# POOL issues eight scatters and then eight gathers, in place of four and four

## What is computed

```python
row, col = src, dst
edge_input = concatenate([x[row], x[col], edge_attr], axis=-1)
h = silu(edge_input @ eW1 + eb1)
m_ij = silu(h @ eW2 + eb2)
agg = segment_sum(m_ij, row, num_segments=50000)
update = silu(concatenate([x, agg]) @ nW1 + nb1) @ nW2 + nb2
out = layernorm(x + (x + update))
```

## Time and profile before

| | |
|---|---|
| median of 3 runs | 1614.44 us (1608.35 to 1617.39) |
| the profiled execution: time, span | 1598.11 us, 1596.6 us |
| mean granted TensorE clock | 0.923 of full speed |
| busy share of the span | PE 82%, DVE 59%, ACT 28%, POOL 65% |
| gathers L340, scatters L381 | 392 and 392 indirect DMAs on POOL, 999 and 1010 ns each |
| edge stage, as the copies of q (L776) stand in the trace | 132.7 to 1254.3 us |

### The profile page before, as it was taken

One profiled execution on the slowest core, in us unless ns is written; L12 is line 12 of the kernel. 1 busy time (PEld: TensorE's weight loads), 2 busy tenths in 40 slices (PEclk: granted clock), 3 DMA queues, 4 the chain that ended last, 5 costly groups with the idle time before them and its releaser, 6 DMA issues.

```text
span 1596.6 us, 24603 instructions
## 1 busy us (share of the span) xinstructions
PE 1304.5 (82%) x7491; PEld 886.1 (56%) x7491; DVE 937.9 (59%) x2976; ACT 443.4 (28%) x766; POOL 1043.0 (65%) x956
## 2 busy tenths in 40 slices
PE   1109888888888888888888888878999699999996
PEld 1005554454454454545455455545666499998995
DVE  9104554554554554554554555546677388888886
ACT  0001111111111111111111111111222177777776
POOL 8763666666666666666666666663443488887885
PEclk9558999999999999999999999998999899999998
DMA  9995333333333333333333333332333499999995
GB/s 379 410 413 172 99 100 106 102 99 101 107 98 102 109 98 106 101 101 105 99 105 101 102 103 102 101 107 81 106 111 94 156 358 383 383 381 365 382 384 227
DMA packets 156842, 284.94 MB, mean 178 GB/s; under 512 B 28046, under 2 KB 92322, under 8 KB 156708
## 3 DMA queue, kind: packets, MB, share of 16 engines
q1 hardware_dynamic: 110020, 162.78, 31.3%
q10 hardware_dynamic: 21600, 68.32, 10.6%
q0 software_dynamic: 25088, 52.23, 10.2%
HBM read 188.31 MB, written 94.91 MB: 177 GB/s over the span
## 4 chain that ended last, share of the span: by engine, by line
PE 31%; DVE 28%; another core or an unknown queue 28%; issue 8%; SPq 4%; DMA 1%; POOL 0%; ACT 0%; ACTq 0%; POOLq 0%
DVE junk L761 14%; PE psum L549 9%; PE psum L559 6%; DVE onehot L753 6%; PE psum L546 5%; DVE pick L743 4%; DVE xsT L734 2%; PE psum L488 2%; PE psum L502 1%; PE psum L505 1%; PE psum L525 1%; SPq L275 1%; PE psum L514 1%; PE psum L530 1%
## 5 line engine op out<-in xcount | busy, mean ns | idle before, releaser
L340 POOL DMA_INDIRECT x_src<-x_d,idx_src x392 | 391.5, 999 | 269.3 <-PE psum L476 149.2
L381 POOL DMA_INDIRECT table<-q,pos x392 | 395.9, 1010 | 199.7 <-issue 113.7
L761 DVE CUSTOM_DVE_ANT_0 junk<-onehot,psum 128x625 f16<-128x625 f16 x392 | 299.1, 800 | 74.2 <-PE psum L505 62.2
L776 DVE COPY q<-psum 128x512 f32<-128x512 f32 x98 | 67.8, 692 | 459.8 <-remote 425.7
L502 PE MATMUL psum<-onehot,after 128*128 128x512 f16 (+1 forms) x780 | 183.9, 320 | 155.1 <-DVE rank L761 153.6
L488 PEld LDWEIGHTS psum<-pick,window 128*128 128x128 f32 x1568 | 201.4, 200 | 95.3 <-issue 95.3
L488 PE MATMUL psum<-pick,window 128*128 128x128 f32 x1568 | 198.7, 282 | 33.7 <-issue 33.7
L502 PEld LDWEIGHTS psum<-onehot,after 128*128 128x128 f16 x780 | 55.2, 100 | 283.0 <-issue 268.8
L505 PE MATMUL psum<-onehot,before 128*128 128x512 f16 (+1 forms) x784 | 187.1, 324 | 0.0
L441 POOL TENSOR_TENSOR rstd<-var_eps,minus_half 128x5 f32<-128x5 f32 (+1 forms) x79 | 134.5, 1703 | 74.0 <-DVE var_eps L821 74.0
L590 ACT ACTIVATE hT<-psum,b_e 128x512 f32<-128x512 f32 x98 | 67.3, 687 | 401.5 <-remote 184.1
(11 more groups left out here) (92 smaller groups left out, 1520.9 us busy)
## 6 DMA issues: line engine op xcount, KB each, us to landing
window<-x_d SPq DMA_DIRECT2D x392, 128.0 KB
slots_in<-table SPq DMA_DIRECT2D x79, 528.0 KB, 6.2
table<-empty ACTq DMA_DIRECT2D x9, 4224.0 KB
x_in<-x_d SPq DMA_DIRECT2D x78, 320.0 KB, 5.1
xT_in<-xT_d SPq DMA_DIRECT2D x78, 320.0 KB, 5.2
out<-y_out ACTq DMA_DIRECT2D x78, 320.0 KB, 5.4
place<-place_dram SPq DMA_DIRECT2D x98, 128.0 KB
x_src<-x_d,idx_src POOLq DMA_INDIRECT x392
```

What stands on the lines that cost most here:

```text
L340: pool.indirect_dma_start(rows, None, x[:, :], bass.IndirectOffsetOnAxis(ap=idx[:, g * TILES + t:g * TILES + t + 1], axis=0)).then_inc(don ...
L381: pool.indirect_dma_start(table[:, :], bass.IndirectOffsetOnAxis(ap=pos[:, g * TILES + t:g * TILES + t + 1], axis=0), q[g % Q][:, t, :], None,
L761: V.tensor_tensor_reduce(out=junk[t % 2][:], in0=onehot[g % 2][:, t, :], in1=p_rank[t % 2], scale=-step if t % 2 else step, scalar=0.0, op ...
```

## The change

In the taken branch POOL goes through the groups in pairs: the scatters of groups g and g + 1, then the gathers of groups g + 22 and g + 23.

```diff
-                for g in range(GROUPS):
-                    scatter(g)
-                    gather_src(g + LEAD)
+                for g in range(0, GROUPS, 2):
+                    for h in range(g, min(g + 2, GROUPS)):
+                        scatter(h)
+                    for h in range(g, min(g + 2, GROUPS)):
+                        gather_src(h + LEAD)
```

## The result

The changed kernel takes 1770.34 us (median of 4 runs, 1767.29 to 1779.0) where the kernel before takes 1612.58 (4 runs): the ratio is 1.0986, with a 95% interval of 1.0935 to 1.1037. It is slower by 158 us; the prediction said 1750, slower by 144.

What follows compares the result with a forecast made beforehand. The prediction took POOL's unbroken runs of indirect DMAs, delaying PE's signals, as the bound. Long and short runs, 39 x 17.5 + 38 x 10.5 = 1081.5 us against 937.4, add 144 us: 1750 us, range 1610 to 1810.

Steps and rivals of the forecast that it cites:

- Issue and moved waits cost nothing: POOL's 392 scatters and 392 gathers are issued as before, and scatters still wait zero for q in the steady part.
- The rhythm of 4 and 12: POOL's one run of eight DMAs per group becomes runs of 4 and of 12 in turn.
- The run of 12 takes 17.5 us: Four gathers and eight scatters 15.31 us, delay to hT 1.87, then 0.30 to the next gather; 39 such runs.
- The run of 4 takes 10.5 us: POOL's short run of four gathers, bounded by 9.1 and 12.0 us, taken as 10.5; 38 such runs.
- The sum: Edge stage from gather 21 to the release: 39 x 17.5 + 38 x 10.5 = 1081.5 us against 937.4, plus 144 us.
- The rule of no contention: Skill rule that only VectorE and GpSimd contend, on their shared port pair; by it POOL's order would cost PE 0.
- The smaller loss: Rival, chance 0.18: clock doesn't fall and release is as after eight; plus 71 us, 1669 or 1685 us.
- The faster rival: Rival, chance 0.12: delay comes from gathers and scatters meeting, which the change halves; 116 us less, 1482 or 1498 us.
- No change: Rival, chance 0.08: POOL's order doesn't matter and a pair keeps 24.06 us; 1598 or 1614 us.
- hold: While POOL issues indirect DMAs unbroken for over some 5 us, PE's finished work reaches other engines late, shortly after the run.

Runs made afterwards that it cites:

- E7: Changed kernel with no scatters, gathers of two groups issued as one run of eight, on the chip where the kernel before takes 1379.14 us: 1339.72 us.
- E12: Same program as E7 (no scatters, gathers in runs of eight), on a chip where the kernel before takes 1591.87 us: 1534.69 us.
- E1: Changed kernel with turns of four groups in place of two, sixteen scatters then sixteen gathers: 1822.86 us, ratio 1.138 to the kernel before.
- E2: Kernel before with its run of eight mixed tile by tile, scatter and gather alternating, the gathers' wait moved ahead: 1644.10 us, ratio 1.0239.
- E5: Changed kernel with window loads for groups 0 to 2 only, on the chip where the kernel before takes 1379.14 us: 1375.00 us, ratio 0.9977.
- E3: Changed kernel with a break of about 1 us (a memset and a wait) in POOL's issuing after every four DMAs: 1641.17 us, ratio 1.0214.
- E8: Kernel before with one break of about 0.6 us between gathers and scatters, on the chip where the kernel before takes 1379.14 us: 1449.63 us, ratio 1.0510.
- E10: Same program as E5 (window loads for groups 0 to 2 only), where the kernel before takes 1594.59 us: 1887.42 us, ratio 1.1839.

## Why the prediction was right, point by point

- **Issue and moved waits cost nothing.** Right. L340 and L381 are issued 392 times each, POOL is busy 1041.5 us in place of 1043.0, and no scatter waits for q in the steady part.
- **The rhythm of 4 and 12.** Right, in each of the 38 pairs.
- **The run of 12 takes 17.5 us.** By the starts of the first gathers of the groups 21 to 97 in POOL's timeline, the mean of 38 is 17.60 (17.5 to 17.7). Its parts: 15.16 us from the first to the last DMA's end (15.31 said), 2.11 to hT (1.87 said), 0.30 to the next gather. hT waits 13 us for a release that isn't found, where some 11 were said. The count of these runs was wrong by one: the last of the 39, with group 97's gathers, goes on to sixteen DMAs as in the earlier trace rows (1243.53 to 1263.79), and from its start to the next gather would be 23.2 us, not 17.5.
- **The run of 4 takes 10.5 us.** This term was sized too low: the mean of 38 is 11.15, from 9.9 to 12.5. The upper end of the bound, 12.0, was passed. The granted clock tells the short ones from the long ones: 22 of the 38 stretches have 0.82 to 0.89 and take 10.5 us on average, as forecast; 16 have 0.73 to 0.78 and take 12.0. Two neighbours:

```profile
254.54:265.16 10.62, 10.62 (x51) 6.48 (x52) 7.94 (x23) 2.34 (x4) 4.05 (x4) 0.84 0.32 87
282.71:294.91 12.20, 11.59 (x51) 7.47 (x52) 8.61 (x25) 2.35 (x4) 4.06 (x5) 0.76 0.30 79
```

  The number of matmuls is the same, PE's busy time is 0.97 us longer at the lower clock, and PE idles 0.61 us more; such an idle stretch of about 0.6 us is in 16 of the 38. The long runs before these two look alike, with PE busy 10.1 us of 17.6, so why the clock stays down longer behind some of them is open.
- **The sum.** The profiled executions are 1777.5 and 1596.6 us of span, 180.9 apart. Gather 21 starts 3.1 us later (151.2, where the earlier trace rows have 148.14). From there to the last group's first gather it is 38 x (17.60 + 11.15) = 1092.3 us in place of 76 x 12.03 = 914.4: 177.9 us. What follows the last group's first gather takes the same to 1 us in both. The forecast's terms give 38 x 28.0 = 1064 for this stretch; the 28 us that are missing are 25 of the short runs and 4 of the long ones. With 6 us for the last run and the 3.1 us of gather 21, which is issued before the change can act, this is the way from the forecast's 144 to the 181 of the traces. Between the medians the loss is 158, between the profiled executions 181, because the one of before lies 14 us under its median and the one of after 9 over its own. That 144 lies so near to 158 is in part luck.
- **The rule of no contention** (the Trainium skill, "SBUF — State Buffer", section "Who interferes with whom") is about the ports of SBUF. ACT's wait here is one for PE's semaphore, so the prediction read more from the rule than it says, and the traces don't contradict it. What they show beside it: by the same programs ACT's wait for PE depends on POOL's run on one chip and doesn't on another; E7 and E12 differ by 4.7 us a pair.
- **The smaller loss** (no fall of the clock, the release as after eight) fell on both counts: the clock in the short runs is 0.73 to 0.89 although PE idles only some 7 us in each long run, and the release takes 2.11 us in place of 1.43.
- **The faster rival** (gathers meeting scatters) fell by E1, E2 and E12. **No change** is what a chip without a hold might give. The changed kernel was not run on it; E5 is the changed kernel without its window loads and takes 1375 there, beside the kernel before with its own at 1379.

What stays open: what it is that keeps PE's signals back, and why not on one chip. Shown is, for the chips that have it, that it comes with POOL's indirect DMAs of either kind, that what it costs grows with the length of the unbroken run, that breaks 0.6 to 0.9 us longer than the usual 0.30, after every four DMAs, take most of it away, and that neither SP's window loads nor a high DMA load are needed. The ends of matmuls are modelled in the profile, so the traces can't tell a late signal from a product that is itself finished late; they show only that PE goes on to its next products meanwhile (turn_src at 733.36, 9 us before hT). No version was found that beats the kernel before.

## What to carry to other kernels

A wait that looks free, because the engine that waits is far from its bound, can be what keeps a neighbour fast: POOL's waits between its runs were when most of PE's signals came through, and taking turns in larger pieces removed them. When an engine idles on a semaphore although the producer's record has ended, look at which other queue is issuing without a break, and at the delay after its run ends, and try a short break; one long run already in the trace, at the end of a stage, can price a change that makes such runs the rule. Compare such kernels on the same chip only.

## What the runs showed of the hardware that was not expected

- The same program took 1379 us on one chip and 1592 to 1608 on three others; the spread on one chip was 14 us at the most. With runs of eight gathers a pair takes 18.2 us on the one and 22.9 on another. On the fast chip 696 indirect DMAs went out in one run (E5), and hT's wait for PE stayed at 4.32 us.
- A loss can be undone by adding work: E3, with memsets in POOL's queue, is 0.0214 over the kernel before where the changed kernel is 0.0986 over it. Where there is no hold the same kind of break costs 5.1% (E8).
- The clock stayed down longer behind some holds than behind others that look the same: 16 of 38 short runs have a granted clock of 0.73 to 0.78, the others 0.82 to 0.89, and that is 1.5 us a run.
- Taking away 128 KB window loads, four a group, made the kernel slower on a chip with the hold (E10: ratio 1.1839 against 1.0973), since it let POOL's run grow from 12 to 16 DMAs.
